# A decoder's self-attention stages: row maxima taken one PSUM bank at a time, with a signal for each bank

## The reference

```python
# 16 heads of 16 channels; for each of the 16 sequences
q, k, v = x @ Wq, x @ Wk, x @ Wv                     # (+ biases in L3_attn)
# L1_xattn: k, v = concat(context keys, k), concat(context values, v)
scores = einsum('bhqd,bhkd->bhqk', q, k) / sqrt(16)
# L1_ffn, L3_attn: scores of later keys are masked
attn = softmax(scores, axis=-1)
out = einsum('bhqk,bhkd->bhqd', attn, v) @ Wo + bo
x = layernorm(x + out)                               # in L1_ffn: x + out, the norm comes later
```

## Time and profile before

| | us |
|---|---|
| median of 3 executions | 3326.37 |
| the three | 3326.37, 3320.43, 12966.53 |
| profiled execution, own time | 3308.19 |
| its span on the core | 3306.4 |
| busy: PE / DVE / ACT / POOL | 2759.3 / 1655.7 / 1426.9 / 1335.7 |

### The profile page before, as it was taken

How to read it: one execution, slowest core, us unless ns; L and a number is a source line. 1 busy time by engine, 2 the same in 40 slices (tenths; PEclk the granted TensorE clock), 3 DMA queues, 4 the chain that set the end, 5 groups by cost and what they waited for, 6 DMA issues and landing times. The chain is left out here.

```text
span 3306.4 us, 71042 instructions
## 1 busy us (share of the span) xinstructions
PE 2759.3 (83%) x25047; PEld 2149.9 (65%) x25105; DVE 1655.7 (50%) x3600; ACT 1426.9 (43%) x4568; POOL 1335.7 (40%) x1553
## 2 busy tenths in 40 slices
PE   5888888559989979938992988999994994998989
PEld 4777776436666657625652766777873673767878
DVE  3898899564446645531115772333331224554633
ACT  3565655344356647713322871333330332772310
POOL 1666666433356655531005661233332003662310
PEclk9999999779989989958996998999995997998999
DMA  3000000210010000051112002000006101002010
GB/s 139 3 2 2 2 2 2 59 34 1 1 38 13 16 15 1 0 194 49 48 42 64 1 1 97 10 10 6 10 1 248 33 29 48 1 1 68 24 36 20
DMA packets 81754, 113.38 MB, mean 34 GB/s; under 512 B 12000, under 2 KB 60129, under 8 KB 81265
## 3 DMA queue, kind: packets, MB, share of 16 engines
q1 hardware_dynamic: 71904, 92.46, 8.4%
q0 software_dynamic: 4608, 12.59, 1.2%
q10 hardware_dynamic: 5008, 5.11, 0.5%
HBM read 88.50 MB, written 21.63 MB: 33 GB/s over the span
## 5 line engine op out<-in xcount | busy, mean ns | idle before, releaser
L714 POOL TENSOR_TENSOR probs<-probs,inv 128x512 f32<-128x512 f32 x320 | 328.0, 1039 | 303.1 <-DVE inv L1042 302.6
L3381 POOL TENSOR_TENSOR hc<-h,bc 128x1024 f32<-128x1024 f32 x128 | 301.7, 2358 | 170.7 <-DVE h L3648 158.5
L938 ACT ACTIVATE probs<-s_ps,negmax 128x128 f32<-128x128 f32 (+1 forms) x768 | 297.1, 415 | 9.6 <-DVE negmax L1002 8.3
L3648 DVE TENSOR_TENSOR_SCAN h<-da,dbu_ps 128x1024 f32<-128x1024 f32 x128 | 292.3, 2283 | 10.4 <-DVE dbu_ps L3660 4.6
L810 PE MATMUL t_ps<-ident,probs 128*128 128x128 f32 x1280 | 209.0, 286 | 53.7 <-POOL probs L714 44.4
L810 PEld LDWEIGHTS t_ps<-ident,probs 128*128 128x128 f32 x1280 | 139.9, 142 | 120.8 <-POOL probs L714 58.2
L3466 PE MATMUL dta_ps<-dt,a_spread 32*128 32x128 f32 x2048 | 157.5, 294 | 44.1 <-ACT da L3594 26.8
L3594 ACT ACTIVATE da<-dta_ps 128x1016 f32<-128x1016 f32 x128 | 130.2, 1017 | 136.1 <-PE dta_ps L3466 135.8
L3660 DVE TENSOR_TENSOR dbu_ps<-dbu_ps,bc 128x1024 f32<-128x1024 f32 x128 | 155.6, 1216 | 55.1 <-PE dbu_ps L3471 54.9
L1002 DVE TENSOR_REDUCE negmax<-s_ps 128x4 f32<-128x1024 f32 (+1 forms) x128 | 156.5, 1223 | 48.1 <-PE s_ps L796 46.2
L3466 PEld LDWEIGHTS dta_ps<-dt,a_spread 32*128 32x128 f32 x2048 | 132.3, 196 | 67.0 <-ACT da L3594 30.2
(11 more groups left out here) (476 smaller groups left out, 6866.7 us busy)
## 6 DMA issues: line engine op xcount, KB each, us to landing
c_in<-in_ctx SPq DMA_DIRECT2D x48, 256.0 KB, 2.7
w_up<-in_L_ffn_w SPq DMA_DIRECT2D x8, 1024.0 KB, 13.5
w_down<-in_L_ffn_w SPq DMA_DIRECT2D x8, 1024.0 KB, 12.4
rows<-expert_rows_in SPq DMA_DIRECT2D x62, 128.0 KB, 2.1
expert_rows_out<-y SPq DMA_DIRECT2D x62, 128.0 KB, 1.7
expert_rows_in<-zeros ACTq DMA_DIRECT2D x1, 4992.0 KB, 28.3
w_gate<-in_L_ffn_w SPq DMA_DIRECT2D x8, 512.0 KB, 9.6
w_up<-in_L_ffn_w SPq DMA_DIRECT2D x8, 512.0 KB, 9.5
```

Source lines behind the costliest of these rows:

```text
L714: pool.tensor_tensor(probs[:, u % 2, i], probs[:, u % 2, i], inv[:, u % 2, HB * i:HB * (i + 1)].unsqueeze(2).broadcast_to([P, HB, W]), ALU ...
L938: last = act.activation(probs[:, u % 2, i, k, :], src, ACT.Exp, bias=negmax[:, u % 2, at], accum_out=sums[:, u % 2, at])
L3381: pool.tensor_tensor(hc[:, s % 4], h[:, s % 2], bc[:, j, 1, :].unsqueeze(1).broadcast_to([P, 2 * G, P]), ALU.mult).then_inc(hc_ready.sem, 1)
L3648: dve.tensor_tensor_scan(flat(h[:, s % 2]), flat(da[:, s % 4]), dbu_ps[s % 2][:, :, :, :].rearrange("p i g t -> p (i g t)"), 0.0, ALU.mult ...
```

## The change

In the three stages without distances `row_max` becomes two `tensor_reduce` instructions, one for each bank of the pair, both behind the same two waits as before, and each signals `negmax_done`. The counter thus goes up by two for a pair, ACT's `exponentiate` waits for the signal of its own bank, and the counter is moved on by twice as much at the end of a stage. The stage with distances already did it so and isn't changed.

```diff
-    MAXES = 2 if alibi else 1
...
                 def exponentiate(b, u, i):
                     g = NP * b + u
-                    act.wait_ge(negmax_done.sem, negmax_done.done(MAXES * g + (i if alibi else 0)))
+                    act.wait_ge(negmax_done.sem, negmax_done.done(2 * g + i))
...
                     else:
-                        scores = s_ps[u % 2][:, :, :].rearrange("p i (k w) -> p (i k) w", w=W)
-                        dve.tensor_reduce(negmax[:, u % 2, :], scores, AX.X, ALU.max, negate=True
-                                          ).then_inc(negmax_done.sem, 1)
+                        for i in range(2):
+                            scores = s_ps[u % 2][:, i, :].rearrange("p (k w) -> p k w", w=W)
+                            dve.tensor_reduce(negmax[:, u % 2, HB * i:HB * (i + 1)], scores, AX.X, ALU.max, negate=True
+                                              ).then_inc(negmax_done.sem, 1)
...
         if alibi:
             biased_done.advance(2 * B * NP)
-            negmax_done.advance(B * NP)
+        negmax_done.advance(B * NP)
```

## The result

The changed kernel takes 3324.88 us in the median (22 executions, 3314.93 to 3331.62), the kernel before 3318.17 us in the same comparison. The ratio is 1.0023 with an interval of 1.0012 to 1.0034, so 7.6 us (4 to 11) slower: within 2%, though not nothing. The forecast was 3327.7 us and +1.3 us, with bounds of -1.6 and +4.5 us. The changed kernel run a second time gave 1.0007 (0.9992 to 1.0021), which is 2.3 us. The two intervals overlap from 1.0012 to 1.0021, 4 to 7 us.

What follows compares the result with a forecast made beforehand. PE was taken as the busiest engine in all three stages, DVE's busy time as bounding nothing. +2.1 us for the delayed `finish` and -0.8 us at stage starts made +1.3 us on 3326.37: 3327.7 us, range 3310 to 3346.

Steps and rivals of the forecast that it cites:

- What the instruction costs what stands behind it: Two reductions delay `finish`, and PE's `project_v`, by 0.08 us, 13 times each in `L1_ffn` and `L3_attn`: +2.1 us.
- The rival that the second reduction is held: DVE starts the second reduction only when the first has ended: +4.2 us instead of +2.1, 3329.8 us; 10%.
- the rule of the Trainium skill that I weighed against the trace: A fixed cost exposed between DVE instructions, so many small tiles pay it each time; (N + 151) cycles for f32 `tensor_tensor`.
- The estimate of 20.1 us by that page: 151 cycles, 0.157 us, more on DVE for each of 128 pairs, if every one was on a path.
- The stage starts: First Exp of `L1_ffn` and `L3_attn` gets its maxima earlier, 0.40 us worth each: -0.8 us; nothing in `L1_xattn`.
- The steady state of the signal: Bank 0's maxima come 0.53 us earlier, but for 124 pairs ACT's copy ends last: nothing gained.
- ACT runs ahead: Rival: ACT really waits for the maxima, so bank 0 starts 0.53 us earlier 128 times: -67.8 us, 3258.5 us; 3%.
- the kept place in `L1_xattn` counts: Rival: one pair's Exp, 0.11 us earlier once a sequence, carries on: -1.8 us on top of the sum, 3325.9 us; 7%.
- The fixed cost is paid in every pair: Rival: DVE's extra 0.161 us is on the path in all 128 pairs: +20.6 us, 3347.0 us; 6%.
- ACT's number of waits stays the same, only their values change; they are worked out while the copy ahead of them runs: On ACT, the changed wait values were given no cost in the sum.
- or grows in `L1_xattn`: Sign that the forecast is wrong: the distance from one sequence to the next grows in `L1_xattn`, where it should stay.
- DVE's cover of 0.47 us: In `L1_xattn`, DVE's least idle gap behind the reduction, 0.47 us, takes in the 0.08 to 0.16 us delay: nothing.

Runs made afterwards that it cites:

- e2: Kernel before with two reductions a pair, only the second signalling once; ACT's program unchanged; ratio 1.0008 to the kernel before.
- e8: Kernel before with four 128x256 reductions a pair, only the last signalling, ACT's program unchanged; ratio 1.0042 to the kernel before.
- e9: The changed kernel run once more, unchanged, against the kernel before; ratio 1.0007.
- e1: The kernel before run once more, nothing changed, against itself; ratio 1.0004.
- e10: The changed kernel, but ACT waits for the second bank's signal before either bank; ratio 1.0021 to the kernel before.
- e3: Kernel before with one reduction raising the counter by two, ACT's wait values as in the changed kernel; ratio 1.0009 to the kernel before.
- e4: Changed kernel with ACT's two waits in `copy_probs` and `copy_turned` swapped, the long one last; ratio 0.9994 to the kernel before.
- e13: Changed kernel with `finish` ahead of the maxima, and PE's `out` ahead of the scores, in the causal stages; ratio 1.0053 to the kernel before.
- e11: Kernel before with `finish` ahead of the maxima, and PE's `out` ahead of the scores, in the causal stages; ratio 1.0045 to the kernel before.
- e12: Kernel before with `finish` ahead of the maxima in the causal stages and ACT's waits in `copy_probs` and `copy_turned` swapped; ratio 1.0035 to the kernel before.
- e7: Kernel before with ACT's two waits in `copy_probs` and `copy_turned` swapped, the long one last; 3314.25 us, ratio 0.9989 to the kernel before.

## Why the prediction was right, and where it was wrong

**The size.** +1.3 us was forecast with bounds from -1.6 to +4.5, and 7.6 us (4 to 11) and 2.3 us (-3 to +7) were measured. The sign is right; of the two measurements the first lies above the bounds. The time, 3324.88 against 3327.7 us, lies in the range, but that is partly luck: the forecast started from the median of three executions, 3326.37, and the kernel before had 3318.17 in the comparison, 8.2 us less, while the change cost more than forecast. The range of 36 us was drawn from how far executions lie apart, and not from the sum. And the sum was right for only part of its reasons.

**What the instruction costs what stands behind it.** Forecast 0.08 us a pair, within 0 and 0.16; it was 0.06, shown by the changed kernel, by e2, and by e8 with three times as much. Its place, `finish` in the two causal stages and from there `project_v`, is shown too. PE's wait grew from 0.28 to 0.33 us, 13 times in each stage:

```profile
PE bank_d L776 <- DVE x L1049: 4.3, 13, 0.3
...
PE bank_d L776 <- DVE y L1052: 4.3, 13, 0.3
```

In the earlier trace rows it was 3.6 and 3.5 us. So +2.1 us was +1.5 (13 x 0.055 + 13 x 0.064). The rival that the second reduction is held falls: its price was 0.16, and a pair of reductions ends at 1.29 us, not at the 1.38 of two that don't overlap.

That also settles how far the rule of the Trainium skill that I weighed against the trace (VectorE: DVE Perf Modes, section on the TRN2 errata) applies here. It says that the latency of SBUF is exposed between instructions, and its (N + 151) cycles are measured for `tensor_tensor`; the reductions here read PSUM. They are 0.685 us each and not half of 1.223, so a fixed cost is there, but what stands behind pays it as 0.06 us for each further one, and not as 151 cycles, and only where it waits for nothing else. The estimate of 20.1 us by that page doesn't hold: e2 has all 128 further reductions and lies at 1.0008 (-2 to +8 us).

**The stage starts.** Forecast -0.8 us as 2 x 0.40; the reciprocals came 0.48 us earlier in both stages (2.31 instead of 2.79 us behind the first reduction's start), so -1.0. In `L1_ffn` this isn't sure: in e9 they stand at 3.71 us, behind a late copy of the keys. In `L1_xattn` nothing was forecast, as that copy comes later, and it is 3.86 us before, 3.93 and 3.70 in the two profiles of the changed kernel. That the copy comes so late there isn't fixed either: in e1, the kernel before once more, the reciprocals stand at 2.31.

**The steady state of the signal.** Right: e10, which takes the signal away, has the same three distances. "ACT runs ahead" (-67.8 us) falls with it. So does "the kept place in `L1_xattn` counts" (-1.8 us). "The fixed cost is paid in every pair" (+20.6 us) falls with e2.

**The step that failed.** "ACT's number of waits stays the same, only their values change; they are worked out while the copy ahead of them runs": nothing was forecast for this, and it is the largest single term. A register operation is done in its turn in the queue, and in `copy_probs` and `copy_turned` its turn comes behind a wait that ACT is held at. There it delays the copy by 0.08 us (0.115 instead of 0.036 us behind the transposes' end). e3, which has only the values, shows the 0.16 us; e2, which has only the reductions, doesn't; e4, which moves the operations ahead of the long wait, gives 0.11 of it back, and the rest stands behind waits that have become instructions of their own. Over 13 to 16 sequences it is +2.1 to +2.5 us. My prediction named it as what would show the forecast wrong ("or grows in `L1_xattn`"), but looked for the cause in DVE's cover of 0.47 us. That cover held.

**The sum.** +1.5 for `finish`, -1.0 for the starts and +2.1 to +2.5 in `L1_xattn` make +2.6 to +3.0 us. From the first to the last reduction of the three changed stages the profiles have 263.19, 178.70 and 168.32 us before and 265.19, 178.84 and 168.43 after: +2.25 us. The second profiles, e1 and e9, have 265.05, 175.78 and 168.35 and 264.96, 177.05 and 168.43: +1.26 us. `L1_ffn` alone differs by 2.9 us between the two profiles of the kernel before, in its first three distances, so that the agreement with the sum says little. The second comparison, 2.3 us, agrees. The first, 4 to 11 us, asks for at least one more. What it is stays open. One place where a part may lie is `L2_attn`, whose program is the same in the kernel before and in e2 and whose distances differ nevertheless, 11.209 and 11.286 us (changed kernel 11.275). It isn't chance from profile to profile: the six profiles with two reductions a pair (the changed kernel, e2, e4, e9, e10, e13) have 11.275 to 11.293, and five with one (before, e1, e3, e11, e12) have 11.202 to 11.211; e4 and e12 have ACT's waits turned round in that stage too. Over 13 sequences that is 0.9 us. Yet e7 has 10.970 with one reduction and e8 10.979 with four, so the number of reductions alone doesn't decide it, and the cause isn't shown. What the profiles show of it stands at the end.

## What to carry to other kernels

When an engine waits for two semaphores, the one that it is usually held at belongs last, and everything worked out for the other one ahead of it: a change of a counter's step can move such a calculation behind the wait, without a line of the diff showing it. Splitting an instruction costs the step from start to start, and only those pay it who stand behind it in its queue on the way to the bound engine. A signal given earlier is worth at most what its receiver really waits for it, and with a bound engine beside it not even that, as the distances of `L3_attn` in e11 and e13 show.

## What the runs showed of the hardware that I had not expected

**An operation on a register in front of an instruction isn't free.** It takes 35 ns in ACT's queue, and behind a wait that ACT is held at it moved the copy by 0.08 us (0.036 to 0.115 us behind the transposes' end). A wait that is an instruction of its own takes 17 ns and moved it by 0.06 us (0.097 in e4).

**A stage that no one changed differs, and PE's clock with it.** Windows over `L2_attn` from its first to its last maxima, for the kernel before, then the changed one, then e8 (length; busy PE, PEld, DVE, ACT, POOL; granted clock):

```profile
1802.72:1972.68 169.96, 151.80 (x1599) 121.18 (x1598) 128.68 (x758) 141.92 (x606) 105.25 (x131) 0.96 0.00 1
```

```profile
1820.69:1993.40 172.71, 153.16 (x1599) 122.77 (x1598) 129.15 (x758) 141.13 (x606) 105.15 (x131) 0.95 0.00 1
```

```profile
1814.17:1982.88 168.71, 148.62 (x1599) 118.50 (x1598) 129.93 (x758) 141.98 (x606) 105.23 (x131) 0.98 0.00 1
```

In these three the stage is the longer, the lower the clock: 168.71 us at 0.98, 169.96 at 0.96, 172.71 at 0.95; the kernel before had 171.34 at 0.95 in its second profile. The clock isn't all of it: at 0.96, with PE busy for 151.7 to 151.8 us, the stage took 169.96 us in the kernel before, 171.25 in e3, 172.15 in e9 and 172.21 in e2. (e7's 167.06 us at 0.99 don't belong here, since its turned waits stand in `L2_attn` too.) Within it there are sequences of 10.85 us, and some of about 12.2 in which PE's projections take 0.213 us for a matmul instead of 0.112, which is the one clock level (1.2 GHz) instead of the other (2.4). These two rows are windows over one of each kind in the kernel before:

```profile
1875.00:1885.00 10.00, 9.04 (x104) 7.47 (x104) 7.88 (x47) 8.36 (x36) 6.99 (x9) 1.00 0.00 0
1886.00:1897.00 11.00, 10.11 (x94) 8.49 (x96) 7.18 (x45) 8.01 (x34) 6.79 (x9) 0.84 0.00 0
```

A stage has three of them in the kernel before and one in e8, and its last distance is 10.0 us in some profiles and 11.6 in others. Together this is worth up to 4 us here, more than half of the 7.6 us that were to be explained. What makes PE lose its level in one sequence and not in the next, the runs don't show.
